# The last pass of a two-layer graph network: one relu moved to the Pool, another cut in four widths, two loads cut in quarters

## What is computed

```
support = x1 @ W[top1]                      # W of the expert chosen for the batch
o       = adj @ support                     # per batch, 1024 x 512
mean, var over all rows of all batches of one expert
y   = relu((o - mean[top1]) * rsqrt(var[top1] + 1e-5) * gamma[top1] + beta[top1])
out = layernorm(x1 + y)                     # over the 512 columns of a row
```

## Time and profile before

| | us |
|---|---|
| median of 3 runs | 902.99 |
| lowest, highest | 902.95, 904.0 |
| the profiled execution | 904.8 |
| its span in the profile | 903.0 |
| start of the last pass's first relu | 821.33 |

### The profile page before, as it was taken

The page is one execution under the profiler, slowest core; times in us unless marked ns, Lnnn a source line. Parts: engine busy times, 40 slices in busy tenths (PEclk is TensorE's granted clock), DMA queues, the critical chain, the costliest instruction groups (busy, mean ns, idle before and its releaser), DMA issues.

```text
span 903.0 us, 12481 instructions
## 1 busy us (share of the span) xinstructions
PE 756.5 (84%) x3922; PEld 356.7 (40%) x3922; DVE 761.8 (84%) x1635; ACT 780.2 (86%) x790; POOL 675.1 (75%) x761
## 2 busy tenths in 40 slices
PE   1544458899999999999999999999999989996561
PEld 1211123344444444444444444444444434344451
DVE  1999988899999999999999999999999942316995
ACT  5999988999999999999999999999999811116995
POOL 6699999999988888888889888888888320000675
PEclk8766669899999999999999999999999999997886
DMA  8799887887787879877877798879766200789899
GB/s 230 207 262 256 198 228 178 219 201 207 200 233 196 190 182 241 205 187 193 233 187 187 187 234 198 197 191 244 195 177 150 61 0 1 263 333 345 324 375 374
DMA packets 262693, 191.18 MB, mean 212 GB/s; under 512 B 210018, under 2 KB 210274, under 8 KB 261090
## 3 DMA queue, kind: packets, MB, share of 16 engines
q1 hardware_dynamic: 262482, 190.38, 77.0%
q10 hardware_dynamic: 144, 0.00, 0.0%
HBM read 91.52 MB, written 48.50 MB: 155 GB/s over the span
## 4 chain that ended last, share of the span: by engine, by line
DVE 50%; POOL 18%; ACT 13%; PE 10%; issue 6%; DMA 2%; SPq 0%; DVEq 0%; POOLq 0%; ACTq 0%
DVE wgt L850 19%; DVE ps_t L882 18%; DVE x_in L869 6%; PE ps_z L1040 5%; ACT ps_t L599 4%; ACT ps_t L597 4%; POOL adj_cut L462 4%; PE ps_o L1056 3%; POOL adj_in L457 2%; POOL x_turn L473 2%; POOL x1p L499 2%; POOL adj_cut L460 2%; PE ps_t L1056 2%; POOL x_in L490 1%; DMA w_sel<-w_planes 1%
## 5 line engine op out<-in xcount | busy, mean ns | idle before, releaser
L1040 PE MATMUL ps_z<-adjT,x1p 128*128 128x512 f16 x1536 | 345.8, 382 | 0.0
L1025 PE MATMUL ps_h<-w0T,x_turn 128*128 128x512 f16 x768 | 195.1, 408 | 72.1 <-DVE x_in L869 54.0
L882 DVE TENSOR_TENSOR ps_t<-ps_t,wgt 128x1024 f32<-128x1024 f32 x192 | 235.9, 1229 | 22.5 <-ACT ps_t L593 17.9
L850 DVE SCALAR_TENSOR_TENSOR wgt<-wgt,ps_t 128x1024 f32<-128x1024 f32 x192 | 224.8, 1215 | 17.0 <-ACT ps_t L599 16.9
L1040 PEld LDWEIGHTS ps_z<-adjT,x1p 128*128 128x128 f16 x1536 | 150.5, 98 | 182.2 <-issue 5.7
L582 ACT ACTIVATE wgt<-adj_in,neg_mu 128x1024 f32<-128x1024 f32 x192 | 205.6, 1133 | 8.2 <-POOL adj_in L457 8.2
L588 ACT ACTIVATE wgt<-wgt 128x3072 f32<-128x3072 f32 x64 | 176.5, 2758 | 0.0
L1056 PE MATMUL ps_o<-zT,w_sel 128*128 128x512 f16 x684 | 160.2, 385 | 4.3 <-DMA w_sel<-w_planes 4.3
L1025 PEld LDWEIGHTS ps_h<-w0T,x_turn 128*128 128x128 f16 x768 | 75.7, 103 | 182.1 <-issue 94.2
L462 POOL TENSOR_TENSOR adj_cut<-adj_in,adj_cut 128x1024 f16<-128x1024 f32 x64 | 136.6, 2134 | 5.3
L1056 PEld LDWEIGHTS ps_o<-zT,w_sel 128*128 128x128 f16 x684 | 67.4, 99 | 87.9 <-DMA w_sel<-w_planes 5.9
(11 more groups left out here) (218 smaller groups left out, 851.9 us busy)
## 6 DMA issues: line engine op xcount, KB each, us to landing
adj_in<-in_adj_dram SPq DMA_DIRECT2D x64, 512.0 KB, 4.0
x_in<-in_x_dram SPq DMA_DIRECT2D x64, 256.0 KB, 4.4
x_spill<-x_in SPq DMA_DIRECT2D x28, 512.0 KB, 3.3
out_spill<-o_stage SPq DMA_DIRECT2D x49, 256.0 KB, 3.0
w_sel<-w_planes SPq DMA_DIRECT2D x8, 1024.0 KB, 5.4
adjT<-x_spill SPq DMA_DIRECT2D x6, 1024.0 KB, 12.4
out_dram<-adjT SPq DMA_DIRECT2D x5, 1024.0 KB, 6.1
adjT<-out_spill SPq DMA_DIRECT2D x4, 1024.0 KB, 12.9
```

The costliest lines, as they stand in the source:

```text
L850: v.scalar_tensor_tensor(out=wgt[:, m % 2, j, :], in0=wgt[:, m % 2, j, :], scalar=SUM_SCALE / W0_SCALE, in1=tot, op0=ALU.mult, op1=ALU.mul ...
L882: v.tensor_tensor(tot, tot, wgt[:, n % 2, j, :], ALU.add).then_inc(dve_tot, 1)
L1025: last = te.matmul(ps_h[:, n % 2, :], xT[:, n % 2, left, c, :], w0T[:, right, c, :], start=(c + i == 0), stop=(c == C - 1 and i == 2))
L1040: last = te.matmul(ps_z[:, u % 2, :], x1p[:, b % 2, left, t, k * P:(k + 1) * P], adjT[:, b % 2, right, t, half * HALF:(half + 1) * HALF], ...
```

## The change

It adds a `relu` to POOL's block that does n = 2 as two instructions a chunk (multiply-add, then max), and takes this relu out of ACT's. ACT's loop is shifted: it does relu(0) and relu(1), the first odd squares and the first 1/std of n = 0, and from then on relu(n + 1) where relu(n) stood, n = 2 left out. relu(0) goes in widths of 128, 128, 256 and 512. `fetch_o(6)` and `fetch_o(7)` load four quarters (two chunks by 512 columns), each pair when 4 or 8 row tiles of the buffer's former batch are transposed.

```diff
--- before.py
+++ after.py
@@ -144,7 +144,7 @@
         act_ln, act_rec, act_z, act_o = (sem(f"act_{k}") for k in ("ln", "rec", "z", "o"))
         act_w0 = sem("act_w0")
         act_bn, act_relu, act_ssq, act_out = (sem(f"act_{k}") for k in ("bn", "relu", "ssq", "out"))
-        pool_small, pool_out = (sem(f"pool_{k}") for k in ("small", "out"))
+        pool_small, pool_out, pool_relu = (sem(f"pool_{k}") for k in ("small", "out", "relu"))
         act_lnv, act_std = sem("act_lnv"), sem("act_std")
         dve_nmr, dve_out = sem("dve_nmr"), sem("dve_out")
 
@@ -244,6 +244,17 @@
 
         def is_even(j):
             return j % 2 == 0 or j >= END_ROWS
+
+
+        BY_POOL = 2
+
+        def relu_done(n):
+
+            return 4 * C + n * C - (C if n > BY_POOL else 0)
+
+        def landed_o(n):
+
+            return o_back[n % RING], 32 if n < RING else 64 + (32 if n % RING else 0)
 
         def std_group(n, half):
 
@@ -383,16 +394,17 @@
                         sp.wait_ge(pe_z, TILES)
                     elif n == 5:
                         sp.wait_ge(pe_o, TILES)
-                    else:
-
-                        sp.wait_ge(pe_back, (n - RING + 1) * T)
-                        wait(sp, *landed(o_back, n - RING))
-
                     for k in range(2):
                         sp.wait_ge(o_stored[k], (b + 1) * T * 8)
+                    src = out_spill.rearrange("b (h c p) n -> b h p c n", h=2, p=P)[b]
+                    if n >= RING:
+                        for at in range(0, NR, HALF):
+                            sp.wait_ge(pe_back, (n - RING) * T + at // P + G)
+                            for h in range(2):
+                                sp.dma_start(o_buf[i][h][:, :, at:at + HALF], src[h][:, :, at:at + HALF]).then_inc(o_back[i], 16)
+                        return
                     for h in range(2):
-                        src = out_spill.rearrange("b (h c p) n -> b h p c n", h=2, p=P)[b, h]
-                        sp.dma_start(o_buf[i][h], src).then_inc(o_back[i], 16)
+                        sp.dma_start(o_buf[i][h], src[h]).then_inc(o_back[i], 16)
 
             def store_y(n):
                 for g in range(2):
@@ -551,6 +563,20 @@
                     g.tensor_scalar(row, row, r_neg[:, n % 4, t:t + 1], r_std[:, n % 4, t:t + 1],
                                     ALU.add, ALU.mult).then_inc(pool_out, 1)
 
+            def relu(n):
+
+                i, b = n % RING, batch_of(n)
+                pool.wait_ge(dve_bn, BN_ALL)
+                pool.wait_ge(*landed_o(n))
+                for k in range(C):
+                    g.tensor_scalar(o_chunk(i, k), o_chunk(i, k), b_sb[:, b, k:k + 1], b_sb[:, b, C + k:C + k + 1],
+                                    ALU.mult, ALU.add).then_inc(pool_small, 1)
+                smalls[0] += C
+                pool.wait_ge(pool_small, smalls[0])
+                for k in range(C):
+                    g.tensor_scalar(o_chunk(i, k), o_chunk(i, k), 0.0, 1.0, ALU.max, ALU.mult).then_inc(pool_relu, 1)
+
+            relu(BY_POOL)
             for n in range(NB):
                 if n in (0, NB - 1):
                     minus_mean(n, 0, G)
@@ -660,6 +686,8 @@
             s.activation(e_sb[:, :, 0:C], e_lnv[:], ACT.Exp, scale=-0.5).then_inc(act_bn, 1)
             act.wait_ge(dve_bn, BN_DONE)
 
+            FIRST_PIECES = [slice(0, P), slice(P, 2 * P), slice(2 * P, HALF), slice(HALF, NR)]
+
             def relu(n, chunks):
 
                 i, b = n % RING, batch_of(n)
@@ -667,11 +695,11 @@
                     act.wait_ge(dve_bn, BN_ALL)
                 if chunks[0] == 0:
                     wait(act, act_o, TILES if n < 2 else 0)
-                    wait(act, *landed(o_back, n))
+                    if n > 0:
+                        act.wait_ge(*landed_o(n))
                 pieces = [slice(0, NR)]
                 if n == 0:
-                    chunks = range(C) if chunks[0] == 0 else ()
-                    pieces = [slice(0, P), slice(P, HALF), slice(HALF, NR)]
+                    pieces = FIRST_PIECES
                 for piece in pieces:
                     for k in chunks:
                         s.activation(o_chunk(i, k)[:, piece], o_chunk(i, k)[:, piece], ACT.Relu,
@@ -708,21 +736,22 @@
                 act.wait_ge(act_lnv, lns[0])
                 s.activation(r_std[:, at, first:last], r_lnv[:, at, first:last], ACT.Exp, scale=-0.5).then_inc(act_std, 1)
 
-            for n in range(NB + 1):
-                if n < NB:
-                    relu(n, (0, 1))
-                if 0 <= n - 2:
-                    odd_squares(n - 2, 1)
-                    inverse_std(n - 2, G if n == 2 else 0, T)
-                if n < NB:
-                    relu(n, (2, 3))
+            relu(0, range(C))
+            relu(1, range(C))
+            odd_squares(0, 0)
+            inverse_std(0, 0, G)
+            for n in range(2, NB + 1):
+                if n + 1 < NB:
+                    relu(n + 1, (0, 1))
+                odd_squares(n - 2, 1)
+                inverse_std(n - 2, G if n == 2 else 0, T)
+                if n + 1 < NB:
+                    relu(n + 1, (2, 3))
                 if n == NB:
                     act.wait_ge(pool_nmr, 1)
                     norm(NB - 2, range(G, T))
-                if 0 <= n - 1:
-                    odd_squares(n - 1, 0)
-                if n in (1, NB):
-                    inverse_std(n - 1, 0, G)
+                odd_squares(n - 1, 0)
+            inverse_std(NB - 1, 0, G)
             inverse_std(NB - 1, G, T)
             act.wait_ge(dve_nmr, 1)
             norm(NB - 1, range(G + G // 2, T))
@@ -1088,12 +1117,12 @@
 
                 for t in range(T):
 
-                    if t == 0:
-                        pe.wait_ge(act_relu, C if n == 0 else C * n + 3 * C)
-                    if n == 0 and t == 1:
-                        pe.wait_ge(act_relu, 2 * C)
-                    if n == 0 and t == G:
-                        pe.wait_ge(act_relu, 3 * C)
+                    if n == 0 and t in (0, 1, 2, G):
+                        pe.wait_ge(act_relu, (min(t, 3) + 1) * C)
+                    if t == 0 and n == BY_POOL:
+                        pe.wait_ge(pool_relu, C)
+                    elif t == 0 and n > 0:
+                        pe.wait_ge(act_relu, relu_done(n))
                     wait(pe, dve_y2, n * T + t - 3)
                     for c in range(C):
                         last = te.transpose(ps_y[t % 4][:, c * P:(c + 1) * P], o_chunk(n % RING, c)[:, t * P:(t + 1) * P],
```

## The result

The changed kernel takes 908.68 us (median of 4 runs, 908.14 to 910.0) against 902.97 before: ratio 1.0062, 95% interval 1.0041 to 1.0084. It is 5.7 us slower; 904.1 was forecast, with 905.4 as the upper end.

A forecast was written before the change was run, and what follows sets the result against it. The transfer queue, nearly level with ACT and POOL's supply, was taken to end last: filling 1.13 later, +0.13 for 2 KB rows, less a 0.15 dry spell, +1.1 on 903.0 gives 904.1 us; range 901.4 to 905.4.

The forecast's parts named there:

- What bounds the kernel: Last pass: two chains of nearly one length, ACT and POOL supplying stores, and the transfer queue with 21 MB to move.
- relu(0) in four widths: On ACT, narrower pieces of relu(0) cost 1.13 us extra; TensorE's tile 1 some 0.8 us sooner buys nothing.
- 1/std of the first half batch not sooner: On ACT, the first 1/std of n = 0 keeps its place in the order and comes 1.13 us later.
- o by quarters: Loads of o in the last pass: 2 KB rows in place of 4 KB cost +0.13 us.
- The 2.1 us that I gave as a bound for each transfer: Quarter loads of o: upper bound if each paid a lone transfer's price, 2 × 2.1 = 4.2 us in all.
- relu(2) on POOL: POOL's eight relu instructions take 9.4 us, 822.3 to 831.7, priced by a 1087 ns tensor-scalar row and hidden in idle time.
- the upper bound for any operation of POOL: POOL's relu: slowest 1024-wide operation, 2134 ns with two tensors; eight at 2.13 make 17.1 us, to 839.4.
- rival 4: POOL's relu takes over 13.1 us and delays the first batch's rows, store and queue: 908.1 us; chance 0.05.
- a first store past 845: Sign in the profile of after that POOL is late; the forecast had that store, n = 0's second half, near 843.7.
- on top of +1.1: The queue's forecast delay at the end, +1.1 us, to which the late POOL's excess of +4.0 was added.
- The supply, −0.63: ACT and POOL near the end: POOL starts n = 5 at 879.45 against 880.08, so last stores gain 0.63 us.

The follow-up runs named there:

- e6: Kernel before with the last batch's o loaded ahead of the first batch's stores: 903.21 us, ratio 0.9998.
- e3: Kernel before with relu(0) in widths 128, 128, 256, 512 alone: 904.53 us, ratio 1.0016.
- e2: Kernel before with the loads of o of the last two batches by quarters alone: 902.64 us, ratio 0.9985.
- e4: Kernel before with only POOL's relu of the third batch and ACT's new order, widths and loads as before: 907.82 us, ratio 1.0054.
- e1: Changed kernel with the max in POOL's relu made an addition: 904.25 us, ratio 1.0006.
- e9: Kernel before with three of the third batch's four relu chunks on POOL (max alone), ACT's order and the loads kept: inside the expected 901 to 901.5 us.
- e8: Kernel before with three of the third batch's four relu chunks on POOL (max alone), last batch's o loaded ahead of the first stores: 899.35 us.

## Why the prediction was wrong

*What bounds the kernel* held. The queue, once it fills, sets the end: the table of the second stores shows it over 7 us. One reading was too strong: before, the share falls below one not only at 896.0. The half microseconds from 847.5 (0.83) and 890.0 (0.86) are below it as well, the latter just as the store of 889.72 is issued, so supply and queue were level there too. e6 bears that out.

*relu(0) in four widths, +1.13 on ACT and at the end*: 1.11 on ACT, and in e3 +0.16% in time and 1.1 us in the pass. It held.

*1/std of the first half batch not sooner*: right, 14.47 us into the pass against 13.36.

*o by quarters, +0.13*: nothing, and perhaps a gain. The 2.1 us that I gave as a bound for each transfer, and the fixed 2.0 us by the Trainium skill's "DMA: Bandwidth & Descriptors", section "Anatomy of one DMA — SWDGE (gpsimd) path", don't show in a full queue (e2: ratio 0.9985). The figure of that section is for transfers issued by gpsimd, and these are issued by SP, so it wasn't a price for them in the first place.

***relu(2) on POOL, "I take 9.4, since the same instruction has a row"* is the step that failed.** It assumed that a POOL instruction costs what its name and size say, whatever its operation. The term measured 19.2 us, not 9.4. The 1087 ns came from a multiply and multiply; the name of the instruction in the profile is the same for max, but the operation isn't in the name, and 3.61 us lies above even the 2.13 that I had taken as the upper bound for any operation of POOL. Four of them bring 14.5 instead of 4.4. The rest is rival 4, "POOL is late", which had 0.05, and whose sign, a first store past 845, is what came (845.99). Its mechanism is the one that the runs show; that its 908.1 lies so near the measured 908.68 is in part luck, since it priced all eight instructions at 2.13, where four take 1.19 and four 3.61. With the measured 3.61 its own sum gives 822.3 + 4 × 1.19 + 4 × 3.61 − 835.4 = 6.1 over, and with its "on top of +1.1" 7.2. The end moved by 6.2. What was too much in it: the rows of the first half do begin 20.73 us into the pass and not 13.74, 7.0 later, but those of the second half only 6.0 later, because POOL used to wait 1.08 us in front of them and no longer does; and it is their store that fills the queue. ACT's four widths, 1.1 by themselves, add nothing while POOL is what is late: the second store stands at 27.20 in e4, without them, and at 27.23 with them. Why e4's pass is all the same 1.0 shorter than the changed kernel's (59.7 from the store to the end, not 60.6) wasn't pursued. Its last batch's first store is issued 1.2 us sooner too (72.30 us into the pass, against 73.46), but behind a full queue that alone should not move the end.

*The supply, −0.63*: e1 lets it be read without the late POOL. Its last batch's first store is issued 891.69 − 818.11 = 73.58 us into the pass, before 895.48 − 821.33 = 74.15. The 0.57 are there (0.69 in the changed kernel itself), and as forecast they are worth nothing, since the queue ends last.

## What to carry to other kernels

A price from a neighbouring row holds for the same operation, not for the same instruction name: before moving work to POOL, time the very operation there, above all where it isn't a multiply or an add. Where a queue of transfers is full to the end, the end is fixed by the moment it fills, so ask of every edit what it does to the first stores. Loads that are due late can go into the hole in front of them, which pays only where the supply of the last stores is ahead too: 1.7 us between e9 and e8 by the medians, nothing in e6. Relief given to an engine should be spent where its next result opens something: three chunks taken off ACT were worth 2.2 us by the medians in e9 (1.3 in the length of its pass), where they brought the early 1/std forward; all four were worth nothing that shows in e1, where the relief came out at the end, behind a full queue (its pass is 83.09 us long, against 82.81 in e3, which has the four widths and leaves all on ACT).

## What the runs showed of the hardware that was not expected

POOL's max on 128x1024 float32 takes 2.78 us alone and 3.63 with a multiply, where add and multiply, or two multiplies, with constants take 1.05 to 1.09 us (means of the groups). The Trainium skill's "GPSIMD Engine Reference", section "4.1 Engine selection", calls one-input elementwise work there "roughly line-rate"; the rows agree for multiply and add (128x512 with scalars from SBUF: 0.75 us on POOL, L563, and 0.69 on DVE, L1023) and not for max, 2.5 to 3.5 times as long. Also, issues on SP took longer in the changed kernel: 2.64 us against 0.51 in the rows above, and this one, a load of 1 MB, 4.32 against 1.02. That the longer backlog of the queue is the cause is not shown.

```profile
853.79 4.32 SPq L442 DMA_DIRECT2D w0T<-x_spill  x1
```

The first stage's length, which no edit touched, was uneven from one profiled execution to the next by 5 us (the pass began between 817.97 and 823.11), as much as the effect under study; between single profiled executions only times from the start of the pass compare.
